# First stage of a decoder layer: rows of three engines' queues put in another order

## The chip, the cores and the metric

The kernel runs on one NeuronCore of a Trainium2 chip. The metric is the time of one execution on the device in microseconds (us). Five engines each work through their own queue of instructions strictly in order, and semaphores tie them together: PE (TensorE: matrix products and transposes), DVE (VectorE), ACT (ScalarE), POOL (GpSimd) and SP (SyncE, which here only issues DMA transfers).

## The reference

One decoder layer in float32 on x of shape (2, 512, 1024). Only its first third bears on the change:

```
h   = (x - mean(x)) / sqrt(var(x) + 1e-5)          # each row of 1024
q   = h @ Wq.T                                      # 32 heads of 128
lat = [h @ Wk_down.T, h @ Wv_down.T]                # 256 + 256 columns, by kv head
k, v = lat[:256] @ Wk_up.T, lat[256:] @ Wv_up.T     # 8 kv heads of 128
x   = x + softmax(causal(q @ k.T / sqrt(128))) @ v @ Wo.T
x   = x + layernorm(x) times a quantised context    # second part
x   = x + routed low-rank FFN of layernorm(x)       # third part
```

## The kernel before

The 1024 rows of x are eight tiles of 128 rows (TT = 8; tile t lies in x_sb[:, t, :]). A float32 operand of a product is kept as two float16 parts, a high and a low one, and a product is three matmuls for each piece of 128 along the contraction (high x high, high x low, low x high; the helper split_product, L1551).

**The first stage** normalises the tiles, turns them and multiplies them with the down projections. For one tile t the steps are:

1. DVE takes statistics (two bn_stats of 512 columns at L1112, then L1114 and L1115, which signals var_done). POOL raises var + eps to the power -1/2 (L618, pow_done). DVE refines that in three steps and makes the bias (ln1_rstd, L1123 to L1131, rstd_done).
2. ACT writes the normalised tile into one of two buffers (ln1_apply, L831, ln_done; it needs the transposes of tile t - 2 behind it).
3. PE turns it with eight transposes into two PSUM banks (columns, L1565, ln_turned).
4. ACT copies the two banks to float16 high parts (columns_hi, ht_hi), and DVE makes the low parts from bank and high part (columns_lo, ht_lo). The tile in the profile is h_b, or wo_in for the first half of the columns of tiles 4 to 7.

**The down projection** has four blocks of weights (DOWN = 4), each 128x1024. ACT makes the high part of block n (down_hi, wo_hi) and DVE the low part (down_lo, wo_lo); both are written to wo_sb. PE walks pairs of tiles: in pair p (tiles 2p and 2p + 1) it makes the product with block hp = 0, 1, 2, 3, each of 24 matmuls of 256 columns. Before hp 0 it waits until the low parts of both tiles are there. In pair 0 it also waits for the low part of each block. The transposes of later tiles are put between: before hp 0 and hp 1 those of tiles 2p + 2 and 2p + 3.

**Latents.** After pairs 0 and 1 the four products of the first batch are whole. For each block ACT (latent_hi, L823) and DVE (latent_lo, L1153) copy them out as float16 parts in four pieces of 64x256 (tile o_t in the profile); pairs 2 and 3 write the same PSUM banks again, so hp n of pair 2 waits for the copy of block n. Block 0 is copied in step t = 5 of the loops of ACT and DVE, blocks 1, 2 and 3 in step t = 6 (down_heads). In the loops before the change the refinement of tile t + 2 stands behind the low parts of tile t, so that of tile 7 stands in step 5.

After this stage come the k and v projections, the first queries, and then eight groups of four heads, in which PE is fed by all the others.

The order in the queues is written out by hand. DVE's and ACT's are the loops over t at the end of their first part, PE's is the loop over pairs.

Of the kernel before, what the change touches and what calls it, by code (L numbers as in the profile page):

```python
# [14 lines left out]
TT = TOK // P  # L15
# [5 lines left out]
HALF = 512  # L21
# [79 lines left out]
DOWN = 4  # L101
# [90 lines left out]
def decoder_layer(nc, x, ctx_in, wq, wdown, wup, wo, a_w, b_w, router_w, keys, quant, ctx_whole, b_whole, kv_whole, out):  # L192
# [8 lines left out]
    with ctx:  # L201
        ps = ctx.enter_context(nc.psum_tensor("ps", [P, 8, HALF], F32))
        x_sb = sb("x_sb", [P, TT, DIM], F32)
# [19 lines left out]
        stats = sb("stats", [P, 3 * TT, 2, 6], F32)  # L223
# [76 lines left out]
        x_loaded = [sem(f"x_loaded{n}") for n in range(TT)]  # L300
# [445 lines left out]
        def _(act):  # L746
# [65 lines left out]
            def columns_hi(t):  # L812
                for j in range(2):
                    act.wait_ge(ln_turned, 2 * t + j + 1)
                    split_hi(h_block(t // QT, j)[:, 0, :, t % QT * P:(t % QT + 1) * P],
                             ps[:, 2 * (t % 2) + j, :].rearrange("p (k n) -> p k n", k=4), ht_hi, S_H)

            def latent_hi(b, hp):
                act.wait_ge(gen_done, b * DOWN + hp + 1)
                for half in range(2):  # L820
                    for j in range(2):
                        src, (hi, _) = latent_views(b, hp, half, j)
                        ins = nc.scalar.activation(hi, src, ACT.Copy, scale=LAT_OUT)  # L823
                ins.then_inc(gen_hi, 1)

            def ln1_apply(t):
                if t >= 2:

                    act.wait_ge(ln_turned, 2 * (t - 1))
                act.wait_ge(rstd_done, t + 1)  # L830
                nc.scalar.activation(hn[:, t % 2, :], x_sb[:, t, :], ACT.Identity, bias=ln_bias[:, t:t + 1],  # L831
                                     scale=rstd1[:, 2, t:t + 1]).then_inc(ln_done, 1)

            def down_hi(n):
                act.wait_ge(down_loaded[n], 16)
                split_hi(wo_sb[:, n, 0, :], down_in[:, n, :], wo_hi, S_W)

            down_hi(0)
            for t in range(2):
                ln1_apply(t)  # L840
            for t in range(TT):
                if t in (5, 6):
                    for hp in down_heads(t):
                        latent_hi(0, hp)
                columns_hi(t)
                if t + 2 < TT:
                    ln1_apply(t + 2)
                if t + 1 < DOWN:
                    down_hi(t + 1)
            def up_split(n):  # L850

                act.wait_ge(up_loaded[n % 3], 16 * (n // 3 + 1))
# [202 lines left out]
            for i in range(0, TT + STEPS_AHEAD):  # L1055
                if 0 <= i - 1 < TT:
                    t = i - 1
# [12 lines left out]
                if 0 <= i - 1 < TT:  # L1070
                    t = i - 1
# [17 lines left out]
                if 0 <= i - 1 < TT:  # L1089
                    t = i - 1  # L1090
# [4 lines left out]
        def _(dve):  # L1095
            newtons = [0]

            def link(ins):
                newtons[0] += 1
                ins.then_inc(newton, 1)  # L1100
                dve.wait_ge(newton, newtons[0])
# [6 lines left out]
            def ln_stats(k, t):  # L1108

                n = k * TT + t  # L1110
                for j in range(2):
                    ins = nc.vector.bn_stats(stats[:, n, j, :], x_sb[:, t, j * HALF:(j + 1) * HALF])  # L1112
                link(ins)
                link(nc.vector.bn_aggr(mean_var[:, n, :], stats[:, n, :, :].rearrange("p a b -> p (a b)")))  # L1114
                nc.vector.tensor_scalar(var_eps[:, n:n + 1], mean_var[:, n, 1:2], EPS, None, ALU.add).then_inc(var_done, 1)  # L1115
                variances[0] += 1
                return variances[0]
# [11 lines left out]
            def ln1_rstd(t, turn):  # L1129
                link(ln_rstd(0, t, turn))  # L1130
                nc.vector.scalar_tensor_tensor(ln_bias[:, t:t + 1], mean_var[:, t, 0:1], -1.0, rstd1[:, 2, t:t + 1],  # L1131
                                               ALU.mult, ALU.mult).then_inc(rstd_done, 1)

            def ln1_stats(t):
                dve.wait_ge(x_loaded[t], 16)
                return ln_stats(0, t)
# [5 lines left out]
            def columns_lo(t):  # L1142
                for j in range(2):
                    dve.wait_ge(ht_hi, 2 * t + j + 1)
                    hi, lo = (h_block(t // QT, j)[:, part, :, t % QT * P:(t % QT + 1) * P] for part in range(2))
                    split_lo(lo, ps[:, 2 * (t % 2) + j, :].rearrange("p (k n) -> p k n", k=4), hi, ht_lo, S_H)

            def latent_lo(b, hp):
                dve.wait_ge(gen_hi, b * DOWN + hp + 1)
                for half in range(2):  # L1150
                    for j in range(2):
                        src, (hi, lo) = latent_views(b, hp, half, j)
                        ins = nc.vector.scalar_tensor_tensor(lo, src, LAT_OUT, hi, ALU.mult, ALU.subtract)  # L1153
                ins.then_inc(gen_read, 1)

            def down_lo(n):
                dve.wait_ge(wo_hi, n + 1)
                split_lo(wo_sb[:, n, 1, :], down_in[:, n, :], wo_sb[:, n, 0, :], wo_lo, S_W)

            turns = {t: ln1_stats(t) for t in range(2)}  # L1160
            for t in range(2):
                ln1_rstd(t, turns[t])
            down_lo(0)
            turns[2] = ln1_stats(2)
            for t in range(TT):
                if t in (5, 6):
                    for hp in down_heads(t):
                        latent_lo(0, hp)
                columns_lo(t)
                if t + 2 < TT:  # L1170
                    ln1_rstd(t + 2, turns[t + 2])
                if t + 1 < DOWN:
                    down_lo(t + 1)
                if t + 3 < TT:
                    turns[t + 3] = ln1_stats(t + 3)
            def block_split(place, slot, number):

                dve.wait_ge(wq_hi, number)
# [364 lines left out]
        def _(pe):  # L1543
# [27 lines left out]
            for pair in range(PAIRS):  # L1571

                b, part = pair // 2, pair % 2
                at = part * 2 * P
                for hp in range(DOWN):
                    if hp < 2 and 2 * pair + 2 + hp < TT:
                        columns(2 * pair + 2 + hp)
                    if hp == 0:
                        pe.wait_ge(ht_lo, 4 * (pair + 1))
                    if pair == 0:  # L1580
                        pe.wait_ge(wo_lo, hp + 1)
                    if b == 1 and part == 0:

                        pe.wait_ge(gen_read, hp + 1)
                    ins = split_product(ps[:, DOWN_BANK[hp], part * 2 * P:(part + 1) * 2 * P],
                                        [(lambda i, k=k: wo_sb[:, hp, i, k * P:(k + 1) * P],
                                          lambda j, k=k: h_block(b, k // 4)[:, j, k % 4, at:at + 2 * P])
                                         for k in range(KT)])
                    if part == 1:
                        ins.then_inc(gen_done, 1)  # L1590
# [349 lines left out]
```

## Time and profile before

| what | value |
|---|---|
| median of 3 runs | 1127.27 us (1125.13 to 1130.5) |
| the profiled execution | 1127.93 us, span in the profile 1126.2 us |
| PE busy | 1078.6 us, 96% of the span |
| DVE, ACT, POOL busy | 904.5, 536.3, 411.7 us |
| mean granted clock of TensorE | 0.991 |
| first stage | from 0 to about 69 us |

The profiled execution is 0.66 us above the median of the runs; 1.73 us of it lie outside the span. "Busy" of PE counts pipelined matmuls, so it tells where PE had work, not how fast it went. A row with x24 is 24 instructions that followed each other. The granted clock is given as a share of 2.4 GHz: 1.00 is 2.4 GHz, 0.50 is 1.2 GHz. In the first 25 us that column reads 1.00 while matmuls of the same shape take twice the time that they take later, so there the durations are what tells the clock.

### The profile page before, as it was taken

What the parts mean: (1) busy time and instruction counts of PE and PEld (TensorE: products, weight loads), DVE (VectorE), ACT (ScalarE), POOL (GpSimd) and SP (SyncE); (2) the same over time, 40 slices, a digit from 0 to 9 for tenths busy, and PEclk for the clock granted to TensorE, in tenths of its full rate; (3) what the DMA queues carried; (4) which work ended last, traced back from release to release, by engine and by line L of the source; (5) the groups of instructions that cost most, each with busy time, mean ns of one, the idle gap of its engine ahead of it and who ended that gap; (6) DMA issues with size and microseconds to landing.
All of it is one profiled execution on the core that took longest, in us unless ns stands there. A gap on an engine that the chain in (4) does not pass through costs nothing.

```text
span 1126.2 us, 19872 instructions
## 1 busy us (share of the span) xinstructions
PE 1078.6 (96%) x6361; PEld 581.5 (52%) x6368; DVE 904.5 (80%) x1868; ACT 536.3 (48%) x1094; POOL 411.7 (37%) x423
## 2 busy tenths in 40 slices
PE   4999988999999999999999999999999989799998
PEld 3876544555555555555555555555555544344554
DVE  6789588988787978888887978788888897867753
ACT  4656366545454545455454445454455460342421
POOL 2049655544343534424453434344243340000000
PEclk9999999999999999999999999999999999899999
DMA  8026146654454545455544544554554576000001
GB/s 310 1 79 231 75 89 155 144 138 100 117 133 112 131 123 135 102 119 131 132 103 121 133 112 112 141 131 102 123 131 98 139 200 211 1 1 38 20 38 56
DMA packets 200865, 128.66 MB, mean 114 GB/s; under 512 B 171376, under 2 KB 173552, under 8 KB 199920
## 3 DMA queue, kind: packets, MB, share of 16 engines
q1 hardware_dynamic: 200816, 128.03, 43.6%
q8 instruction: 28, 0.46, 0.2%
q14 instruction: 21, 0.17, 0.1%
HBM read 68.23 MB, written 17.83 MB: 76 GB/s over the span
## 4 chain that ended last, share of the span: by engine, by line
PE 81%; DVE 10%; ACT 5%; issue 2%; DMA 1%; POOL 0%; SPq 0%; ACTq 0%; DVEq 0%; POOLq 0%
PE ps L1551 77%; PE ps L1802 2%; ACT prob L975 1%; DVE stats L1112 1%; DVE wo_sb L1104 1%; DVE h_b L1104 1%; DVE prob L1310 1%; DVE x_sb L1486 1%; DVE x_sb L1468 1%; DVE prob_t L1104 1%; DMA o_t<-in_wdown 1%; ACT prob L1034 1%; PE ps L1565 0%; ACT q_t L1049 0%; ACT side_out L1039 0%
## 5 line engine op out<-in xcount | busy, mean ns | idle before, releaser
L712 POOL TENSOR_SCALAR prob<-prob,row_inv 128x128 f32<-128x128 f32 (+3 forms) x256 | 203.5, 815 | 438.7 <-DVE row_inv L1281 438.7
L1551 PE MATMUL ps<-wo_sb,o_t 128*128 128x512 f16 x1536 | 353.0, 380 | 3.6 <-DVE x_sb L1292 3.6
L1551 PE MATMUL ps<-h_b,wq_sb 128*128 128x512 f16 x1524 | 343.2, 381 | 0.0
L975 ACT ACTIVATE prob<-prob,neg_max 128x128 f32<-128x128 f32 (+3 forms) x256 | 140.6, 550 | 221.7 <-DVE neg_max L1316 221.7
L1551 PEld LDWEIGHTS ps<-h_b,wq_sb 128*128 128x128 f16 x1524 | 148.9, 98 | 179.2 <-issue 3.7
L1551 PEld LDWEIGHTS ps<-wo_sb,o_t 128*128 128x128 f16 x1536 | 147.6, 98 | 173.1 <-DVE x_sb L1292 6.3
L1292 DVE SCALAR_TENSOR_TENSOR x_sb<-ps,x_sb 128x512 f32<-128x512 f32 x256 | 174.0, 685 | 54.9 <-PE ps L1551 54.1
L1551 PE MATMUL ps<-prob_t,v_sb 128*128 128x128 f16 (+2 forms) x960 | 116.4, 274 | 5.6 <-DMA prob_t<-prob_s 5.6
L1551 PE MATMUL ps<-k_t,q_t 128*128 128x512 f16 (+3 forms) x768 | 114.8, 299 | 1.9 <-DVE neg_max L1316 1.8
L1310 DVE CUSTOM_DVE_ANT_0 prob<-ps,mask 128x512 f32<-128x512 f32 (+3 forms) x256 | 110.2, 483 | 2.3 <-issue 1.6
L1551 PEld LDWEIGHTS ps<-prob_t,v_sb 128*128 128x128 f16 x960 | 83.4, 98 | 35.9 <-DMA prob_t<-prob_s 6.5
L748 ACT ACTIVATE q_t<-q_tmp 128x512 f16<-128x512 f32 x60 | 37.8, 630 | 131.7 <-DVE q_tmp L1268 131.7
L1268 DVE SCALAR_TENSOR_TENSOR q_tmp<-ps,q_tmp 128x512 f32<-128x512 f32 x105 | 72.0, 686 | 29.9 <-PE ps L1551 27.4
L1104 DVE SCALAR_TENSOR_TENSOR prob_s<-prob,prob_s 128x1280 f16<-128x1280 f32 x64 | 95.0, 1484 | 0.1
L1551 PEld LDWEIGHTS ps<-k_t,q_t 128*128 128x128 f16 x768 | 66.9, 98 | 53.0 <-issue 2.3
L748 ACT ACTIVATE prob_s<-prob 128x1280 f16<-128x1280 f32 x64 | 80.6, 1259 | 27.6 <-POOL prob L712 27.6
L1104 DVE SCALAR_TENSOR_TENSOR wq_sb<-wq_in,wq_sb 128x512 f16<-128x512 f32 x94 | 67.4, 731 | 0.5 <-ACT wq_sb L748 0.5
L742 POOL TENSOR_TENSOR rstd<-var_eps,minus_half 128x1 f32<-128x1 f32 x16 | 8.8, 550 | 155.3 <-DVE var_eps L1115 155.3
L1104 DVE SCALAR_TENSOR_TENSOR q_t<-q_tmp,q_t 128x512 f16<-128x512 f32 x60 | 62.1, 1056 | 0.7 <-ACT q_t L748 0.7
L1104 DVE SCALAR_TENSOR_TENSOR o_t<-ps,o_t 128x512 f16<-128x512 f32 x64 | 44.2, 691 | 20.1 <-ACT o_t L748 20.1
L748 ACT ACTIVATE wq_sb<-wq_in 128x512 f16<-128x512 f32 x94 | 56.5, 618 | 3.0 <-POOL wq_in L671 3.0
L975 ACT ACTIVATION_READ_ACCUMULATOR prob<-prob,neg_max 128x1 f32 x256 | 47.8, 187 | 0.0
(141 smaller groups left out, 1175.0 us busy)
## 6 DMA issues: line engine op xcount, KB each, us to landing
wq_in<-in_wq SPq DMA_DIRECT2D x64, 256.0 KB, 3.4
wo_in<-in_wo SPq DMA_DIRECT2D x32, 512.0 KB, 3.8
side_in<-in_ctx SPq DMA_DIRECT2D x16, 512.0 KB, 4.4
kv_parts<-wo_sb SPq DMA_DIRECT2D x7, 1024.0 KB, 5.7
x_sb<-in_x SPq DMA_DIRECT2D x8, 512.0 KB, 9.0
ctx_quantised<-side_out SPq DMA_DIRECT2D x16, 256.0 KB, 2.9
h_b<-ctx_quantised SPq DMA_DIRECT2D x2, 2048.0 KB, 10.8
out<-x_sb SPq DMA_DIRECT2D x8, 512.0 KB, 2.6
```

What stands on the lines that cost most here:

```text
L712: ins = nc.gpsimd.tensor_scalar(at, at, row_inv[:, u % 2, q:q + 1], S_P, ALU.mult, ALU.mult)
L748: nc.scalar.activation(dst, src, ACT.Copy, scale=scale).then_inc(signal, 1)
L975: ins = nc.scalar.activation(at, at, ACT.Exp, bias=neg_max[:, n % 2, q:q + 1], scale=SOFTMAX, accum_out=row_sum[:, n % 2, q:q + 1])
L1034: nc.scalar.activation(hn[:, t % 2, :], x_sb[:, t, :], ACT.Identity, bias=x_bias[:, t:t + 1], scale=x_scale[:, 1, t:t + 1]).then_inc(x_aff ...
L1104: nc.vector.scalar_tensor_tensor(dst, src, scale, hi, ALU.mult, ALU.subtract).then_inc(signal, 1)
L1112: ins = nc.vector.bn_stats(stats[:, n, j, :], x_sb[:, t, j * HALF:(j + 1) * HALF])
L1268: nc.vector.scalar_tensor_tensor(q_tmp[:, dst, :], ps[:, Q_BANK[product % 2], :], Q_OUT, q_tmp[:, src, :], ALU.mult, ALU.add).then_inc(com ...
L1292: nc.vector.scalar_tensor_tensor(at, ps[:, bank, :], WO_OUT, at, ALU.mult, ALU.add).then_inc(wo_read, 1)
L1310: ins = nc.vector.tensor_tensor_reduce(prob[:, u % 2, at:at + width], ps[:, at // HALF, at % HALF:at % HALF + width], mask[:, SEQ - width: ...
L1468: nc.vector.scalar_tensor_tensor(x_sb[:, t, :], column_term[:, b, :], row_term[:, t:t + 1], x_sb[:, t, :], ALU.add, ALU.add).then_inc(x_fo ...
L1551: ins = nc.tensor.matmul(out_, lhs(i), rhs(j), start=start and n == 0, stop=stop and n == 3 * len(pairs) - 1)
L1802: ins = nc.tensor.matmul(ps[:, x_banks(t)[j], :], x_qt[:, t % 2, k * P:(k + 1) * P], ctx_q[:, b, k, j * HALF:(j + 1) * HALF], start=k == 0 ...
```

## The change

On DVE the statistics can now be taken in halves (ln1_half, ln1_end). The statistics of tile 1 are split around the refinement of tile 0. Behind the low part of down block 0 stand one half of the statistics of tile 2 and then the low parts of tiles 0 and 1; the rest of tile 2, tile 3 and the blocks 1 to 3 follow. From tile 4 on DVE's loop refines tile t + 1 (before: t + 2) ahead of the low parts of tile t, and takes the statistics of tile t + 2 (before: t + 3). ACT's queue is put in the order that goes with it: tile 0 is normalised ahead of the high part of down block 0, and from step 4 on tile t + 1 is normalised ahead of the high parts of tile t. PE makes the first down product of pair 0 before it turns tile 2, and turns tile 3 ahead of hp 2. No arithmetic is added or taken away.

```diff
@@ -835,18 +835,26 @@
                 act.wait_ge(down_loaded[n], 16)
                 split_hi(wo_sb[:, n, 0, :], down_in[:, n, :], wo_hi, S_W)
 
+            ln1_apply(0)
             down_hi(0)
-            for t in range(2):
-                ln1_apply(t)
-            for t in range(TT):
+            ln1_apply(1)
+            columns_hi(0)
+            columns_hi(1)
+            down_hi(1)
+            ln1_apply(2)
+            down_hi(2)
+            columns_hi(2)
+            ln1_apply(3)
+            down_hi(3)
+            columns_hi(3)
+            ln1_apply(4)
+            for t in range(4, TT):
                 if t in (5, 6):
                     for hp in down_heads(t):
                         latent_hi(0, hp)
+                if t + 1 < TT:
+                    ln1_apply(t + 1)
                 columns_hi(t)
-                if t + 2 < TT:
-                    ln1_apply(t + 2)
-                if t + 1 < DOWN:
-                    down_hi(t + 1)
             def up_split(n):
 
                 act.wait_ge(up_loaded[n % 3], 16 * (n // 3 + 1))
@@ -1111,6 +1119,9 @@
                 for j in range(2):
                     ins = nc.vector.bn_stats(stats[:, n, j, :], x_sb[:, t, j * HALF:(j + 1) * HALF])
                 link(ins)
+                return ln_variance(n)
+
+            def ln_variance(n):
                 link(nc.vector.bn_aggr(mean_var[:, n, :], stats[:, n, :, :].rearrange("p a b -> p (a b)")))
                 nc.vector.tensor_scalar(var_eps[:, n:n + 1], mean_var[:, n, 1:2], EPS, None, ALU.add).then_inc(var_done, 1)
                 variances[0] += 1
@@ -1157,22 +1168,46 @@
                 dve.wait_ge(wo_hi, n + 1)
                 split_lo(wo_sb[:, n, 1, :], down_in[:, n, :], wo_sb[:, n, 0, :], wo_lo, S_W)
 
-            turns = {t: ln1_stats(t) for t in range(2)}
-            for t in range(2):
-                ln1_rstd(t, turns[t])
+            def ln1_half(t, j):
+                dve.wait_ge(x_loaded[t], 16)
+                return nc.vector.bn_stats(stats[:, t, j, :], x_sb[:, t, j * HALF:(j + 1) * HALF])
+
+            def ln1_end(t):
+                link(ln1_half(t, 1))
+                return ln_variance(t)
+
+            ln1_half(0, 0)
+            turns = {0: ln1_end(0)}
+            ln1_half(1, 0)
+            ln1_rstd(0, turns[0])
+            turns[1] = ln1_end(1)
+            ln1_rstd(1, turns[1])
             down_lo(0)
-            turns[2] = ln1_stats(2)
-            for t in range(TT):
+            ln1_half(2, 0)
+            columns_lo(0)
+            columns_lo(1)
+            turns[2] = ln1_end(2)
+            ln1_half(3, 0)
+            ln1_rstd(2, turns[2])
+            down_lo(1)
+            turns[3] = ln1_end(3)
+            down_lo(2)
+            ln1_rstd(3, turns[3])
+            columns_lo(2)
+            down_lo(3)
+            turns[4] = ln1_stats(4)
+            columns_lo(3)
+            ln1_rstd(4, turns[4])
+            turns[5] = ln1_stats(5)
+            for t in range(4, TT):
                 if t in (5, 6):
                     for hp in down_heads(t):
                         latent_lo(0, hp)
+                if t + 1 < TT:
+                    ln1_rstd(t + 1, turns[t + 1])
                 columns_lo(t)
                 if t + 2 < TT:
-                    ln1_rstd(t + 2, turns[t + 2])
-                if t + 1 < DOWN:
-                    down_lo(t + 1)
-                if t + 3 < TT:
-                    turns[t + 3] = ln1_stats(t + 3)
+                    turns[t + 2] = ln1_stats(t + 2)
             def block_split(place, slot, number):
...
@@ -1573,8 +1608,9 @@
                 b, part = pair // 2, pair % 2
                 at = part * 2 * P
                 for hp in range(DOWN):
-                    if hp < 2 and 2 * pair + 2 + hp < TT:
-                        columns(2 * pair + 2 + hp)
+                    turned_here = 2 * pair + 2 + hp - (pair == 0)
+                    if (1 <= hp <= 2 if pair == 0 else hp < 2) and turned_here < TT:
+                        columns(turned_here)
                     if hp == 0:
                         pe.wait_ge(ht_lo, 4 * (pair + 1))
                     if pair == 0:
```

DVE, from the low part of down block 0 (wo_sb) on; h_b are low parts of turned tiles, BN_STATS are halves of the statistics. Before:

```order
L1104 SCALAR_TENSOR_TENSOR wo_sb<-o_t,wo_sb 128x1024
L1112 BN_STATS stats<-x_sb 128x6 x2
L1114 BN_AGGR mean_var<-stats 128x2
L1115 TENSOR_SCALAR var_eps<-mean_var 128x1
L1104 SCALAR_TENSOR_TENSOR h_b<-ps,h_b 128x4x128 x2
L1123 TENSOR_TENSOR rstd1<-rstd0 128x1
L1124 TENSOR_SCALAR rstd1<-rstd1,var_eps 128x1
L1126 SCALAR_TENSOR_TENSOR rstd1<-rstd1,rstd0 128x1
L1131 SCALAR_TENSOR_TENSOR ln_bias<-mean_var,rstd1 128x1
L1104 SCALAR_TENSOR_TENSOR wo_sb<-o_t,wo_sb 128x1024
```

And the same place now:

```order
L1112 SCALAR_TENSOR_TENSOR wo_sb<-o_t,wo_sb 128x1024
L1173 BN_STATS stats<-x_sb 128x6
L1112 SCALAR_TENSOR_TENSOR h_b<-ps,h_b 128x4x128 x4
L1173 BN_STATS stats<-x_sb 128x6
L1125 BN_AGGR mean_var<-stats 128x2
L1126 TENSOR_SCALAR var_eps<-mean_var 128x1
L1173 BN_STATS stats<-x_sb 128x6
L1134 TENSOR_TENSOR rstd1<-rstd0 128x1
L1135 TENSOR_SCALAR rstd1<-rstd1,var_eps 128x1
L1137 SCALAR_TENSOR_TENSOR rstd1<-rstd1,rstd0 128x1
L1142 SCALAR_TENSOR_TENSOR ln_bias<-mean_var,rstd1 128x1
L1112 SCALAR_TENSOR_TENSOR wo_sb<-o_t,wo_sb 128x1024
```

The low parts of both first tiles (x4) now stand together and ahead of the variance of tile 2; before, those of tile 1 stood another block, another tile's statistics and a refinement later.

DVE, steps 5 and 6 of its loop; o_t x4 are the latents of block 0, o_t x12 those of blocks 1 to 3, wo_in and h_b the low parts of a tile, rstd1 and ln_bias a refinement. Before:

```order
L1153 SCALAR_TENSOR_TENSOR o_t<-ps,o_t 64x4x64 x4
L1104 SCALAR_TENSOR_TENSOR wo_in<-ps,wo_in 128x4x128
L1104 SCALAR_TENSOR_TENSOR h_b<-ps,h_b 128x4x128
L1123 TENSOR_TENSOR rstd1<-rstd0 128x1
L1124 TENSOR_SCALAR rstd1<-rstd1,var_eps 128x1
L1126 SCALAR_TENSOR_TENSOR rstd1<-rstd1,rstd0 128x1
L1131 SCALAR_TENSOR_TENSOR ln_bias<-mean_var,rstd1 128x1
L1153 SCALAR_TENSOR_TENSOR o_t<-ps,o_t 64x4x64 x12
```

And now, from the low parts of tile 5 on:

```order
L1112 SCALAR_TENSOR_TENSOR wo_in<-ps,wo_in 128x4x128
L1112 SCALAR_TENSOR_TENSOR h_b<-ps,h_b 128x4x128
L1120 BN_STATS stats<-x_sb 128x6 x2
L1125 BN_AGGR mean_var<-stats 128x2
L1126 TENSOR_SCALAR var_eps<-mean_var 128x1
L1164 SCALAR_TENSOR_TENSOR o_t<-ps,o_t 64x4x64 x12
L1134 TENSOR_TENSOR rstd1<-rstd0 128x1
L1135 TENSOR_SCALAR rstd1<-rstd1,var_eps 128x1
L1137 SCALAR_TENSOR_TENSOR rstd1<-rstd1,rstd0 128x1
L1142 SCALAR_TENSOR_TENSOR ln_bias<-mean_var,rstd1 128x1
```

The refinement of tile 7 stood ahead of the twelve latent pieces and now stands behind them. On ACT the normalising of tile 7 (L831) has moved likewise:

```order
L748 ACTIVATE wo_in<-ps 128x4x128
L748 ACTIVATE h_b<-ps 128x4x128
L823 ACTIVATE o_t<-ps 64x4x64 x12
L831 ACTIVATE prob<-x_sb,ln_bias,rstd1 128x1024
L748 ACTIVATE wo_in<-ps 128x4x128
L748 ACTIVATE h_b<-ps 128x4x128
```

These are the rows of the changed kernel: tile 5's high parts, the latents, tile 7 normalised, tile 6's high parts. Before, L831 stood ahead of the twelve o_t.

## Rows read from the trace of the kernel before

**Rows 1.** the page: its first line, and the chain that ended last by line

```profile
span 1126.2 us, 19872 instructions
...
PE ps L1551 77%; PE ps L1802 2%; ACT prob L975 1%; DVE stats L1112 1%; DVE wo_sb L1104 1%; DVE h_b L1104 1%; DVE prob L1310 1%; DVE x_sb L1486 1%; DVE x_sb L1468 1%; DVE prob_t L1104 1%; DMA o_t<-in_wdown 1%; ACT prob L1034 1%; PE ps L1565 0%; ACT q_t L1049 0%; ACT side_out L1039 0%
```

**Rows 2.** the waits, 0 to 62 us: engine, line, releaser; us in total, times, longest

```profile
ACT prob L831 <- DVE ln_bias L1131: 17.7, 6, 3.9
...
PE ps L1565 <- ACT prob L831: 11.6, 2, 9.9
```

**Rows 3.** timeline, 0 to 10 us: start us, us, engine, line, operation, count [idle before]

```profile
5.97 0.56 POOL L618 TENSOR_TENSOR rstd<-var_eps,minus_half 128x1 f32<-128x1 f32 x1 [2.07 <-DVE var_eps L1115]
...
7.52 1.06 ACT L748 ACTIVATE wo_sb<-o_t 128x1024 f16<-128x1024 f32 x1 [5.51 <-DMA o_t<-in_wdown]
...
8.49 2.36 ACT L831 ACTIVATE prob<-x_sb,ln_bias,rstd 128x1024 f32<-128x1024 f32 x2
...
9.86 3.64 PE L1565 MATMUL ps<-ident,prob 128*128 128x128 f32 x16 [9.86 <-ACT prob L831]
```

**Rows 4.** timeline, 16 to 26 us

```profile
16.17 1.23 DVE L1104 SCALAR_TENSOR_TENSOR wo_sb<-o_t,wo_sb 128x1024 f16<-128x1024 f32 x1 [2.32 <-ACT wo_sb L748]
17.32 1.28 DVE L1112 BATCH_NORM_STATS2 stats<-x_sb 128x6 f32<-128x512 f32 x2
...
18.94 1.28 DVE L1104 SCALAR_TENSOR_TENSOR h_b<-ps,h_b 128x512 f16<-128x512 f32 x2
19.10 0.55 POOL L618 TENSOR_TENSOR rstd<-var_eps,minus_half 128x1 f32<-128x1 f32 x1 [6.73 <-DVE var_eps L1115]
20.14 0.15 DVE L1123 TENSOR_TENSOR rstd<-rstd 128x1 f32<-128x1 f32 x1
...
20.28 4.90 PE L1551 MATMUL ps<-h_b,wo_sb 128*128 128x256 f16 x24 [3.06 <-DVE h_b L1104]
...
21.02 1.24 ACT L831 ACTIVATE prob<-x_sb,ln_bias,rstd 128x1024 f32<-128x1024 f32 x1 [3.91 <-DVE ln_bias L1131]
22.16 1.04 ACT L748 ACTIVATE wo_sb<-o_t 128x1024 f16<-128x1024 f32 x1
23.11 1.06 ACT L748 ACTIVATE h_b<-ps 128x512 f16<-128x512 f32 x2
...
25.01 1.04 PE L1565 MATMUL ps<-ident,prob 128*128 128x128 f32 x8
```

**Rows 5.** timeline of PE alone, 38 to 52 us

```profile
38.58 8.02 PE L1551 MATMUL ps<-h_b,wo_sb 128*128 128x256 f16 x72
46.44 1.04 PE L1565 MATMUL ps<-ident,prob 128*128 128x128 f32 x8
...
49.94 1.04 PE L1565 MATMUL ps<-ident,prob 128*128 128x128 f32 x8
50.81 1.47 PE L1551 MATMUL ps<-wo_in,wo_sb 128*128 128x256 f16 x12
```

**Rows 6.** timeline, 40 to 54 us: latents on DVE

```profile
41.70 1.73 DVE L1153 SCALAR_TENSOR_TENSOR o_t<-ps,o_t 64x256 f16<-64x256 f32 x4 [1.18 <-ACT o_t L823]
...
48.26 5.25 DVE L1153 SCALAR_TENSOR_TENSOR o_t<-ps,o_t 64x256 f16<-64x256 f32 x12 [2.81 <-ACT o_t L823]
```

**Rows 7.** timeline of PE alone, 168 to 190 us

```profile
170.93 2.97 PE L1551 MATMUL ps<-prob_t,v_sb 128*128 128x128 f16 x15 [2.97 <-DMA prob_t<-prob_s]
173.69 5.90 PE L1551 MATMUL ps<-h_b,wq_sb 128*128 128x512 f16 x24
...
183.29 1.81 PE L1551 MATMUL ps<-prob_t,v_sb 128*128 128x128 f16 x15 [2.07 <-DMA prob_t<-prob_s]
184.94 5.34 PE L1551 MATMUL ps<-h_b,wq_sb 128*128 128x512 f16 x24
```

**Rows 8.** windows: busy by engine (count), granted clock, DMA share, GB/s

```profile
170.90:173.70 2.80, 2.77 (x16) 1.77 (x17) 2.10 (x3) 0.82 (x2) 2.80 (x3) 0.59 0.65 246
...
983.20:986.00 2.80, 2.80 (x8) 0.92 (x7) 2.63 (x9) 0.20 (x1) 0.62 (x2) 0.50 0.00 0
```

## The prediction

> **What bounds the kernel now.** I read the page first. Its span is 1126.2 us and 77% of the chain that ended last is one line of matmuls [rows 1], so PE sets the time nearly everywhere, and a microsecond that PE starts later or earlier is kept unless something absorbs it. Then the waits of the first 62 us: PE waits 11.6 us for its first normalised tiles, and ACT waits six times, 17.7 us in all, for the bias that DVE makes [rows 2]. So early on PE is fed by a relay DVE, POOL, DVE, ACT, PE. The timeline shows the relay. Products start at 20.28 us, after an idle of 3.06 us, when the second low part of tile 1 is done (18.94 + 1.28); that low part stands behind a down block and the statistics of tile 2 [rows 4]. Later PE leads: from 38.58 us it runs 72 matmuls, then transposes, without a wait, and turns tile 7 at 49.94 us with no idle before it [rows 5].
>
> **Prices, from one row to the next on the same engine** [rows 4]. DVE: low part of a down block 1.15 us (16.17 to 17.32), statistics with variance 1.62 (17.32 to 18.94), low parts of a tile 1.20 (18.94 to 20.14). From the first step of a refinement to the start of the normalising on ACT 0.88 (20.14 to 21.02); DVE itself is free about 0.1 earlier than that, so 0.75. POOL: the power ends 0.71 after the instruction that follows the variance has begun (18.94 to 19.65). ACT: normalising 1.24 long, 1.14 to the next; high part of a block 0.95. Latents: 1.7 per block on DVE, 5.1 to 5.25 for three [rows 6]. PE: eight transposes step by 0.87 (49.94 to 50.81), a product of 24 matmuls by 2.62 ((46.44 - 38.58) / 3) [rows 5]; at the slow clock 1.82 (3.64 / 2) [rows 3] and 4.9 [rows 4].
>
> **Part 1, the start: the first product comes about 5.8 us earlier.** The power of tile 0 is there at 5.97 + 0.56 = 6.53; DVE now refines at once and ACT normalises at about 7.45. Before, it stood behind the high part of block 0 and began at 8.49 [rows 3]. The refinement pushes the statistics of tile 1 back; its variance comes at about 8.4, its power at 9.0, and it is normalised at about 9.95 (before 8.49 + 1.14 = 9.63). PE turns tile 0 from 8.8 (before 9.86) and tile 1 from 11.2 to 13.1. The low parts of tiles 0 and 1 follow at once and end at about 14.45. First product: 14.5 instead of 20.28.
>
> **Part 2, pairs 0 and 1: 4.6 us are kept.** The first product goes at the slow clock, 14.5 to 19.4, as it did before (4.90 us, 204 ns a matmul) [rows 4]. With tiles 2 and 3 turned (2 x 0.87) and three products at 2.62, pair 0 ends at about 29.0. DVE's queue meanwhile: rest of tile 2 and half of tile 3 to 15.5, power 16.1, tile 2 normalised 17.0; block 1 to 18.0; variance 3 by 19.1; block 2 from 19.25 (it waits for ACT) to 20.4; refinement 3, tile 3 normalised 21.3; low parts of tile 2 to 22.3; block 3, whose high part ACT makes only behind tile 3, 23.5 to 24.65 (a DVE wait of 1.2); statistics of tile 4 to 26.25; low parts of tile 3 to 27.45; tile 4 normalised 28.3 to 29.6. So PE waits 0.6 us for tile 4, turns it at 29.7, and begins pair 1 at 30.5; with tile 5 turned in it pair 1 ends at 30.5 + 0.87 + 4 x 2.62 = 41.85. Before it ended at 46.44. That is 4.6 us.
>
> **Part 3, tile 7: a new wait takes it back.** DVE's refinement of tile 7 now stands behind the latents of blocks 1 to 3, and ACT's normalising likewise. I follow DVE on: statistics 5 to 29.8, power 30.5, tile 5 normalised 31.4; its high parts queue behind that on ACT, 32.6, so the low parts of tile 4 run 33.2 to 34.4 (a wait of 1.9); statistics 6 to 36.0; latents of block 0 to 37.7; refinement 6, tile 6 normalised 38.6 to 39.85; only then high parts of tile 5, and low parts from 40.4 to 41.6 (again 1.9); statistics 7 to 43.2; twelve latent pieces to 48.3; refinement 7 and the hand-over 0.88; tile 7 normalised 49.2 to 50.45. PE turns it at 50.6. PE has meanwhile turned tile 6 and made the first product of pair 2, and stands idle from about 45.35: **5.2 us**. Behind this wait stand seven products of the stage and all that follows. The transposes of tile 7 began at 49.94 before [rows 5], so the first stage is then 0.6 to 0.8 us late, not 4.6 early; I take **+0.7**. The error of the walk is that of some 25 hand-overs rounded to 0.05; I allow 0.7 on either side.
>
> **Part 4, the clock.** After an idle of 2.97 us at 168 to 170.93 PE was slow: 15 matmuls took 2.97 us, which took 1.81 at 183.29 behind an idle of 2.07, and the next 24 took 5.90 against 5.34 [rows 7]; the granted clock was 0.59 in that stretch and 0.50 from 983.2 to 986 [rows 8], which is 1.2 GHz. That cost 1.16 + 0.56 = 1.7 us. The first product lost 4.90 - 2.62 = 2.3 us. The new idle is longer than either of the idles before them. Lower bound of its price: 0, if the clock stays. Upper: 3.2, tile 7 at 1.82 instead of 0.87 and one whole product at 4.9 instead of 2.62. I take 2.0, between the two measured losses. The Trainium skill, "TensorE: Matmul & The Clock Gate", section "Part 4: PE-mode transpose", says that the full clock does not engage for transposes. The trace disagrees: eight transposes took 1.04 us at 25.01 [rows 4] and half of 3.64 in [rows 3]. By the rule the turning of tile 7 would be no cheaper at the fast clock and the price would lose 0.95; I go by the rows.
>
> **What is hidden.** The low parts of tile 7 end at about 53.4, ahead of pair 3, so PE doesn't wait there. The splitting of statistics costs nothing: same instructions, and DVE has the waits named above. No DMA is moved, and the transfers of x are hardly wanted earlier: the statistics of tile 3 begin at 15.5 us instead of 17.32 [rows 4]. Nothing behind the stage waits on an absolute time: k, v and queries start from the latents of PE's last products.
>
> **Sum.** -5.8 at the start, +1.2 by pair 1 (the wait for tile 4 and the other order), +5.3 at tile 7, +2.0 for the clock: **+2.7 us**. Against the profiled execution's own 1127.93 us that is 1130.6; the median of the runs lies 0.66 below it, so 1130.0 us on that scale, 0.24% more.
>
> **Rivals.**
> - The wait comes but the clock stays: +0.7, 1128.0. For it: the idle of 2.07 us at 183.29 left the clock alone [rows 7]. Against: this one is over twice as long.
> - Absorbed: DVE, whose work on tile 7 is done 2.5 us earlier than before, and later stages make good what PE lost; about 0, 1127.3. For it: in the relay of the softmax PE waits for DMA, not for itself (2.97 and 2.07 us) [rows 7]. Against: those transfers start from scores that PE computed, so they move with it.
> - No wait at tile 7, the start's gain is kept: -4.6 plus nothing, 1122.7. It needs PE to get tile 7 by 45.35, that is DVE and ACT 5 us faster over three tiles. The twelve latent pieces alone are 5.1 us of queue, so only a mistake of mine in the queues gives this.
> - The other side, clearly slower: the clock stays low over many products after the wait. At half clock every microsecond of old work costs one more, so from 5 us of work (two products) on the loss with the wait passes 5.7 us and the time 1133. For it: at 983 to 986 the clock was still 0.50 well into the work [rows 8]. Against: the first product ended it within 4.9 us [rows 4]. A slow clock that lasts into the transposes of tile 2 adds up to 0.95 too, of which 0.2 is slack.
>
> **Chances.** Forecast (wait and clock, 1129 to 1132) 0.58; clock stays 0.12; absorbed 0.15; gain kept 0.06; long slow clock 0.09. An effect under 0.5% (5.6 us) can't be told from no change here. The forecast, clock-stays and absorbed cases all lie within it, and so does most of the gain-kept case (4.6 us): same 0.89. The long slow clock is mostly beyond: slower 0.08. Faster 0.03. The range 1125.8 to 1133.0 holds the first three cases with the runs' own spread (1125.13 to 1130.5) and the near end of the fourth, and leaves the ends of the others out.
>
> **What would show it.** Right: products start near 14.5 us; the last of pair 1 ends near 42; a wait PE <- ACT prob (normalising) of about 5 us ends near 50.6; transposes and matmuls behind it take twice the usual time; the k and v stage, which began at 50.81 + 7 x 2.62 = 69.15 [rows 5], begins near 71.9. Wrong in part 1: first product after 16. Wrong in part 3: a wait under 3 us, or the refinement of tile 7 done before 46. Wrong in part 4: 24 matmuls behind the wait in 2.8 us. Wrong in "hidden": PE's stage ends 2.7 late but the span does not grow by it.

## The result, and the profile after

The changed kernel takes 1129.49 us in the median of 20 runs (1128.19 to 1131.62), the kernel before 1127.41 us (1125.07 to 1130.63, 20 runs). The ratio is 1.0019 with a 95% interval of 1.0011 to 1.0028: 2.1 us slower, between 1.2 and 3.2. The forecast was 2.7 us slower, 1130.0 us. The interval excludes zero, so 20 runs did tell an effect that the prediction held for too small to be told, and it excludes the +0.7 us of the rival in which the clock stays.

The page's first line and the chain by line answer to [rows 1]; the products' share of the chain has fallen from 77% to 76%.

```profile
span 1127.5 us, 19879 instructions
...
PE ps L1586 76%; PE ps L1838 2%; DVE stats L1120 2%; ACT prob L983 1%; DVE h_b L1112 1%; DVE prob L1345 1%; DVE wo_sb L1112 1%; DVE o_t L1164 1%; DVE x_sb L1503 1%; ACT prob L831 1%; DVE x_sb L1521 1%; ACT prob L1042 1%; DVE prob_t L1112 1%; ACT side_out L1047 1%; ACT q_t L1057 0%
```

The waits of the first 62 us answer to [rows 2] (engine, line, releaser; us in total, times, longest). PE waits 16.7 us for normalised tiles where it waited 11.6, and six times instead of twice. The third line is new among the large ones: DVE waits for high parts that ACT makes.

```profile
ACT prob L831 <- DVE ln_bias L1142: 22.4, 8, 5.3
PE ps L1600 <- ACT prob L831: 16.7, 6, 8.7
...
DVE wo_in L1112 <- ACT wo_in L748: 5.8, 3, 2.0
```

PE's timeline answers to the PE rows of [rows 3 to 5]. The columns are start, us, engine, line, operation, count, and in brackets the idle time before it and what ended it.

```profile
8.69 1.94 PE L1600 MATMUL ps<-ident,prob 128*128 128x128 f32 x8 [8.69 <-ACT prob L831]
11.10 1.77 PE L1600 MATMUL ps<-ident,prob 128*128 128x128 f32 x8 [0.47 <-ACT prob L831]
14.28 2.79 PE L1586 MATMUL ps<-h_b,wo_sb 128*128 128x256 f16 x24 [1.42 <-DVE h_b L1112]
18.11 1.09 PE L1600 MATMUL ps<-ident,prob 128*128 128x128 f32 x8 [1.03 <-ACT prob L831]
...
22.36 1.09 PE L1600 MATMUL ps<-ident,prob 128*128 128x128 f32 x8 [0.54 <-ACT prob L831]
...
29.43 1.09 PE L1600 MATMUL ps<-ident,prob 128*128 128x128 f32 x8 [0.74 <-ACT prob L831]
...
33.85 8.02 PE L1586 MATMUL ps<-h_b,wo_sb 128*128 128x256 f16 x72
41.71 1.04 PE L1600 MATMUL ps<-ident,prob 128*128 128x128 f32 x8
...
50.64 1.97 PE L1600 MATMUL ps<-ident,prob 128*128 128x128 f32 x8 [5.27 <-ACT prob L831]
52.40 2.02 PE L1586 MATMUL ps<-wo_in,wo_sb 128*128 128x256 f16 x12
54.25 1.47 PE L1586 MATMUL ps<-h_b,wo_sb 128*128 128x256 f16 x12
...
71.28 1.03 PE L1586 MATMUL ps<-o_t,prob_t 128*128 128x512 f16 x4
```

The first product begins at 14.28 instead of 20.28 us. Tiles 2, 3 and 4 are waited for (1.03, 0.54, 0.74). Tile 6 is turned at 41.71 instead of 46.44: PE is 4.7 us ahead. Then it is idle for 5.27 us and turns tile 7 at 50.64 instead of 49.94, 0.70 late. The transposes take 1.97 us instead of 1.04, the next twelve matmuls step by 1.85 instead of 1.31, and k and v begin at 71.28 instead of 69.15, **2.13 us late**.

What DVE and ACT do meanwhile (timeline of all engines, answers to [rows 6]):

```profile
32.98 0.69 DVE L1112 SCALAR_TENSOR_TENSOR wo_in<-ps,wo_in 128x512 f16<-128x512 f32 x1 [1.85 <-ACT wo_in L748]
...
40.35 0.69 DVE L1112 SCALAR_TENSOR_TENSOR wo_in<-ps,wo_in 128x512 f16<-128x512 f32 x1 [1.99 <-ACT wo_in L748]
...
43.18 5.24 DVE L1164 SCALAR_TENSOR_TENSOR o_t<-ps,o_t 64x256 f16<-64x256 f32 x12
...
48.45 0.16 DVE L1134 TENSOR_TENSOR rstd<-rstd 128x1 f32<-128x1 f32 x1
...
49.34 1.24 ACT L831 ACTIVATE prob<-x_sb,ln_bias,rstd 128x1024 f32<-128x1024 f32 x1 [3.97 <-DVE ln_bias L1142]
```

DVE waits 1.85 and 1.99 us for the high parts of tiles 4 and 5, makes twelve latent pieces in 5.24 us, and only then refines tile 7. ACT, which has been idle for 3.97 us, normalises it at 49.34.

The windows tell the clock (busy time of PE, PEld, DVE, ACT and POOL with counts, then granted clock, DMA share, GB/s):

```profile
45.20:50.40 5.20, 0.17 (x2) 0.00 (x0) 3.80 (x12) 1.23 (x2) 0.00 (x0) 0.97 0.00 0
...
50.80:53.00 2.20, 2.20 (x11) 1.99 (x12) 1.76 (x3) 1.85 (x4) 0.00 (x0) 0.50 0.00 0
```

Behind the idle the granted clock is 0.50, that is 1.2 GHz, as in [rows 8].

**Where the 2.1 us are after that.** Late in the program, with the same work in both kernels, the kernel before:

```profile
927.95 7.04 PE L1551 MATMUL ps<-wo_sb,o_t 128*128 128x512 f16 x24 [2.41 <-DVE x_sb L1292]
```

```profile
976.22 1.32 PE L1888 MATMUL ps<-ident,k_t 128*128 128x128 f32 x8 [3.40 <-ACT k_t L1066]
```

and the changed one:

```profile
931.79 5.35 PE L1586 MATMUL ps<-wo_sb,o_t 128*128 128x512 f16 x24 [2.41 <-DVE x_sb L1327]
```

```profile
978.39 1.91 PE L1924 MATMUL ps<-ident,k_t 128*128 128x128 f32 x8 [3.40 <-ACT k_t L1074]
```

The last rows of each (the first transposes for the routed part) stand 2.17 us apart, nearly the 2.13 of the start of k and v. It did not stay at that in between, and the near equality is luck: two events of the clock cancel. At 183 us the lag was 2.15 (185.44 against 183.29 in [rows 7]). There the changed kernel ran slow where the kernel before did not (2.29 and 6.59 us where that took 1.81 and 5.34), and it lost another 1.7:

```profile
185.44 2.29 PE L1586 MATMUL ps<-prob_t,v_sb 128*128 128x128 f16 x15 [2.16 <-DMA prob_t<-prob_s]
187.52 6.59 PE L1586 MATMUL ps<-h_b,wq_sb 128*128 128x512 f16 x24
```

So the rows at 928 and 932 stand 3.84 us apart. There it is the other way round: behind the same idle of 2.41 us the kernel before ran 24 matmuls mostly at the slow clock (7.04 us), the changed one at the fast clock (5.35). Of the eight kernels below, five ran them fast in the profiled run and three slow. Apart from these two events the lag of 2.1 us is carried through 900 us. The two spans differ by only 1.3 us, as near 995 us the clock differs once more; the 20 runs each give 2.1.

### The profile page after: what moved, and what is told of

Its sections match the earlier page's. It is cut to its first block, busy times and chain, and to the rows that moved or that the text cites. A ratio compares the mean times of both kernels' runs of the same rounds, so it can differ in the third digit from the quotient of the medians.

```text
span 1127.5 us, 19879 instructions
## 1 busy us (share of the span) xinstructions
PE 1077.5 (96%) x6368; PEld 580.8 (52%) x6368; DVE 905.2 (80%) x1868; ACT 536.8 (48%) x1094; POOL 411.1 (36%) x423
## 4 chain that ended last, share of the span: by engine, by line
PE 79%; DVE 12%; ACT 5%; issue 2%; POOL 1%; DMA 0%; ACTq 0%; DVEq 0%; POOLq 0%; SPq 0%
PE ps L1586 76%; PE ps L1838 2%; DVE stats L1120 2%; ACT prob L983 1%; DVE h_b L1112 1%; DVE prob L1345 1%; DVE wo_sb L1112 1%; DVE o_t L1164 1%; DVE x_sb L1503 1%; ACT prob L831 1%; DVE x_sb L1521 1%; ACT prob L1042 1%; DVE prob_t L1112 1%; ACT side_out L1047 1%; ACT q_t L1057 0%
## 5 line engine op out<-in xcount | busy, mean ns | idle before, releaser
L1112 DVE SCALAR_TENSOR_TENSOR wq_sb<-wq_in,wq_sb 128x512 f16<-128x512 f32 x94 | 67.6, 733 | 0.5 <-ACT wq_sb L748 0.3
```

Of the source, the lines that this page charges most:

```text
L1112: nc.vector.scalar_tensor_tensor(dst, src, scale, hi, ALU.mult, ALU.subtract).then_inc(signal, 1)
```

## The experiments

All were timed in five rounds beside the kernel before. "k and v" is the start of the k and v projections in the profiled run, 69.15 us before and 71.28 with the change; a ratio is to the kernel before on the same chip. A ratio is not the quotient of the two medians: for the best kernel the ratio says 4.6 us less and the medians 3.7. A landmark is that of one profiled run. Before any wait that an edit touches it moves by itself: in the seven traces that have the change's start and PE's new order (the change among them) the first product begins between 14.21 and 14.59 us, so differences under 0.4 us are not read from one landmark.

| kernel | idle at tile 7, us | k and v, us | median, us | ratio (95%) |
|---|---|---|---|---|
| the change | 5.27 | 71.28 | 1129.49 | 1.0019 (1.0011 to 1.0028) |
| DVE refines tile 7 first | 1.30 | 66.25 | 1123.47 | 0.9974 (0.9964 to 0.9984) |
| and ACT: tile 7 between latents | 0.74 | 65.56 | 1123.23 | 0.9962 (0.9951 to 0.9974) |
| the wait filled with matmuls | 0.88 | 70.10 | 1128.03 | 1.0010 (0.9996 to 1.0024) |
| before, tile 7 moved alone | 2.06 | 71.29 | 1130.77 | 1.0029 (1.0014 to 1.0044) |
| tile 7 ahead of all latents | 0.73 | 69.11 | 1125.21 | 0.9997 (0.9987 to 1.0007) |
| tile 7 between, high parts first | none | 64.34 | 1122.23 | 0.9959 (0.9946 to 0.9972) |
| the change, high parts first | 2.26 | 68.74 | 1123.75 | 0.9981 (0.9972 to 0.9989) |
| the change, old PE order | 4.22 | 75.00 | 1130.96 | 1.0042 (1.0029 to 1.0055) |

The first four experiments ran beside a kernel before of 1126.98 us, the other four beside one of 1125.9; ratios compare across the two groups, medians do not.

### Take the new wait away: DVE alone

```diff
             for t in range(4, TT):
+                if t == 6:
+                    ln1_rstd(7, turns[7])
                 if t in (5, 6):
                     for hp in down_heads(t):
                         latent_lo(0, hp)
-                if t + 1 < TT:
+                if t + 1 < TT and t != 6:
                     ln1_rstd(t + 1, turns[t + 1])
```

> The changed kernel, and on DVE alone the refinement of tile 7 put ahead of the latents of blocks 1 to 3 (ACT as in the change). Theory (the new wait at tile 7 is what took the head start back): ACT normalises tile 7 as soon as its own latents are done, about 45.3 us; PE turns tile 7 at about 46.6 behind an idle of about 1.3 us instead of 5.3, the clock stays, k and v begin near 68 instead of 71.3 us, and the time is 3 to 3.5 us below the kernel before (about 1124.2) and 5 to 5.5 below the change. Rival (the later stages don't carry a head start, DVE sets their pace): the wait goes, k and v begin earlier, but the time is within 1 us of the kernel before. Rival (the loss lies in the new start itself): as slow as the change, 1129.5.

Measured: 0.26% below the kernel before (2.9 us), 0.45% below the change. PE's timeline:

```profile
46.98 1.09 PE L1602 MATMUL ps<-ident,prob 128*128 128x128 f32 x8 [1.30 <-ACT prob L831]
...
66.25 1.46 PE L1588 MATMUL ps<-o_t,prob_t 128*128 128x512 f16 x6
```

The idle is 1.30 us, as expected, and the turning is at 46.98 (46.6 expected; this run began 0.3 us later); the clock stays (transposes 1.09). k and v begin at 66.25 us, where the expectation said 68: that number was a slip, since 3 us less than 69.15 is 66. Four instructions of refinement in another place of one queue are worth 5 us, 1.4 of it the clock. The rival by which later stages don't carry a head start falls, and so does the one that puts the loss in the new start.

### And ACT between the latents

```diff
                     for hp in down_heads(t):
+                        if hp == 3:
+                            ln1_apply(7)
                         latent_hi(0, hp)
-                if t + 1 < TT:
+                if t + 1 < TT and t != 6:
                     ln1_apply(t + 1)
```

> As the run before, and on ACT tile 7 is normalised ahead of the latents of block 3 instead of behind them. Theory: tile 7 is turned at about 46.2, idle about 0.8 us, k and v begin near 67.6, and the time is 3.6 to 4 us below the kernel before (about 1123.7), 0.5 below the run before. Rival (head start not carried): within 1 us of the kernel before.

```profile
44.10 0.16 DVE L1136 TENSOR_TENSOR rstd<-rstd 128x1 f32<-128x1 f32 x1 [0.66 <-POOL rstd L618]
...
44.82 5.24 DVE L1166 SCALAR_TENSOR_TENSOR o_t<-ps,o_t 64x256 f16<-64x256 f32 x12
45.00 1.24 ACT L831 ACTIVATE prob<-x_sb,ln_bias,rstd 128x1024 f32<-128x1024 f32 x1 [1.02 <-DVE ln_bias L1144]
...
46.29 1.09 PE L1604 MATMUL ps<-ident,prob 128*128 128x128 f32 x8 [0.74 <-ACT prob L831]
```

DVE waits only for POOL's power, refines tile 7 at 44.10, and makes the twelve latent pieces behind that; ACT normalises at 45.00, PE turns the tile at 46.29. k and v begin at 65.56, 3.6 us before the kernel before (the 67.6 of the expectation has the same slip). The ratio 0.9962 is 4.3 us less (2.9 to 5.5). The 0.5 us expected against the run before can't be told from the times, as the intervals overlap; the timelines show 0.69, of which 0.12 is an earlier start.

### Fill the wait

```diff
+                    if pair == 2 and hp == 1:
+                        pe.wait_ge(ht_lo, 12)
+                        for n in range(40):
+                            nc.tensor.matmul(ps[:, 3, 0:2 * P], wo_sb[:, 0, 0, 0:P], h_b[:, 0, 0, 0, 0:2 * P],
+                                             start=True, stop=True)
                     if (1 <= hp <= 2 if pair == 0 else hp < 2) and turned_here < TT:
                         columns(turned_here)
```

> The changed kernel with 40 extra matmuls of 256 columns on PE in the wait for tile 7, into the bank that its transposes write afterwards; nobody reads what they write. They take about 4.4 us (40 x 0.109) of the 5.3 us of idle. Theory (of the 2.1 us that the change lost, 0.7 is lateness of tile 7 and 1.4 the slow clock behind the idle): tile 7 is turned at the same 50.6 us but in 1.04 instead of 1.97 us, the first 24 matmuls behind it take 2.8, k and v begin near 69.9, and the time is 0.7 above the kernel before (about 1128.1), 1.4 below the change. Rival (the clock is not what slows it there): no less than the change, 1129.5.

```profile
45.42 4.53 PE L1615 MATMUL ps<-h_b,wo_sb 128*128 128x256 f16 x40
50.83 1.09 PE L1600 MATMUL ps<-ident,prob 128*128 128x128 f32 x8 [0.88 <-ACT prob L831]
51.76 1.47 PE L1586 MATMUL ps<-wo_in,wo_sb 128*128 128x256 f16 x12
...
70.10 1.46 PE L1586 MATMUL ps<-o_t,prob_t 128*128 128x512 f16 x6
```

```profile
45.20:50.40 5.20, 4.75 (x44) 4.00 (x41) 4.00 (x12) 1.23 (x2) 0.00 (x0) 1.00 0.00 0
...
50.80:53.00 2.20, 2.17 (x20) 2.03 (x21) 1.57 (x3) 2.20 (x5) 0.00 (x0) 1.00 0.05 11
```

Tile 7 comes just as late (50.83, in a run whose first product began 0.2 us later), but its transposes take 1.09 us and the next matmuls step at full speed; the granted clock is 1.00 in both windows in which the change showed 0.97 and 0.50. k and v begin at 70.10, 0.95 us late instead of 2.13. The ratio is 1.1 us above the kernel before (0.5 fewer to 2.7 more), which can't separate the expected 0.7 from 0, nor from the 2.1 of the change: by time alone the rival (the clock is not what slows it) stands. What decides is the rows: with the wait filled the slow matmuls are gone, and in the change the lag at k and v splits into lateness and clock, 2.13 = 0.70 + 1.43.

### Only tile 7, in the kernel before

```diff
@@ ACT
+                if t == 6:
+                    ln1_apply(7)
                 columns_hi(t)
-                if t + 2 < TT:
+                if t + 2 < TT and t != 5:
                     ln1_apply(t + 2)
@@ DVE
+                if t == 6:
+                    ln1_rstd(7, turns[7])
                 columns_lo(t)
-                if t + 2 < TT:
+                if t + 2 < TT and t != 5:
                     ln1_rstd(t + 2, turns[t + 2])
```

> The kernel before with one thing of the change: DVE refines and ACT normalises tile 7 behind the latents of blocks 1 to 3. Theory (the order alone makes the wait): without the head start the latents of block 3 wait for PE; tile 7 is normalised at about 50.7 and turned at about 52.1 us behind an idle of about 2.2 us, k and v begin 2.0 to 2.3 us later than before, near 71.3, plus up to 1.5 if the clock falls; time 1129.4 to 1131. Rival (the wait comes from the other moves, not from this one): as before, 1127.4.

```profile
15.10 1.09 PE L1569 MATMUL ps<-ident,prob 128*128 128x128 f32 x8 [1.75 <-ACT prob L831]
...
52.02 1.09 PE L1569 MATMUL ps<-ident,prob 128*128 128x128 f32 x8 [2.06 <-ACT prob L831]
52.95 1.47 PE L1555 MATMUL ps<-wo_in,wo_sb 128*128 128x256 f16 x12
...
71.29 1.46 PE L1555 MATMUL ps<-o_t,prob_t 128*128 128x512 f16 x6
```

Idle 2.06, turned at 52.02, k and v at 71.29: 2.14 us late, nearly the same as the whole change. The parts differ, so the near equality is chance: here it is all lateness, as the clock stayed behind this idle, and there it is 0.70 of lateness and 1.43 of clock. The one move is enough to lose as much as the whole change, and the rest of the change makes a gain that it hides.

By the ratio this kernel is 3.3 us slower (1.6 to 5.0). The profiled run is not typical of it: it took 1127.43 us, one of three at 1127.2 to 1127.6, while the other nine took 1129.4 to 1132.8. Its lag is still 2.4 us at 928 (its matmuls there begin at 930.36) and goes only behind that, first of all where the kernel before took 7.04 us for the 24 matmuls and this one 5.35. Whether the clock fell behind the wait in the nine slower runs is not shown; the trace is of another run.

### Tile 7 ahead of all latents

```diff
@@ ACT; DVE as in the first experiment
+                if t == 6:
+                    ln1_apply(7)
                 if t in (5, 6):
                     for hp in down_heads(t):
                         latent_hi(0, hp)
-                if t + 1 < TT:
+                if t + 1 < TT and t != 6:
                     ln1_apply(t + 1)
```

> The changed kernel with tile 7's refinement on DVE and its normalising on ACT both put ahead of all three latents of step 6, which is the old order at that place. Theory (the wait moves to whoever stands behind tile 7): tile 7 is turned at about 46.3 us, but ACT makes the high latents of block 1 only behind it, 46 to 47.6, DVE the low ones to 49.3, and PE waits about 2.4 us for block 1 ahead of the second product of pair 2. k and v begin near 68, 1.2 us before the kernel before; time about 1126. Rival (whatever takes tile 7 out of the way of PE gives the whole head start): as in the run with tile 7 between blocks 2 and 3, 1123.2.

```profile
46.27 1.09 PE L1604 MATMUL ps<-ident,prob 128*128 128x128 f32 x8 [0.73 <-ACT prob L831]
49.47 2.74 PE L1590 MATMUL ps<-wo_in,wo_sb 128*128 128x256 f16 x12 [2.11 <-DVE o_t L1166]
```

The wait moves as expected: 0.73 us at tile 7, then 2.11 us for the latents of block 1, whose high parts stand behind tile 7 on ACT. What the expectation left out is the clock: the twelve matmuls behind it took 2.74 us instead of 1.47, and the 24 of that product 1.3 us more than usual. k and v begin at 69.11, not 68, and the ratio is 0.9997 (within 1.5 us of the kernel before): the whole head start is gone again.

### High parts first, with tile 7 between and alone

```diff
+                columns_hi(t)
                 if t + 1 < TT and t != 6:
                     ln1_apply(t + 1)
-                columns_hi(t)
```

> The best version so far (DVE refines tile 7 ahead of the latents, ACT normalises it ahead of block 3's) and on ACT the high parts of tile t ahead of the normalising of tile t + 1 in steps 4 to 7. Theory: the two waits of DVE for high parts (1.85 and 1.99 us) go, tile 7 is normalised at about 42 us, and PE has no wait for it (0.74 before); k and v begin near 64.8 us, the time is 0.7 to 0.8 below that version (about 1122.4). Rival (nothing left there): 1123.2. Theory of a loss (tile 5 to 7 are normalised later and PE waits for them): a PE wait of over 1 us in pair 1 or 2 and over 1124.

```profile
45.12 1.04 PE L1604 MATMUL ps<-ident,prob 128*128 128x128 f32 x8
...
64.34 1.46 PE L1590 MATMUL ps<-o_t,prob_t 128*128 128x512 f16 x6
```

PE turns tile 7 at 45.12 without a wait and k and v begin at 64.34 us, 4.8 earlier than in the kernel before. The ratio 0.9959 (4.6 us less, 3.2 to 6.1, from five runs) is the lowest of all; against the version without this edit (0.9962) the intervals can't tell it apart, the timeline gains 1.2 us, 0.9 of it the gap ahead of tile 7 and most of the rest an earlier start (14.21 instead of 14.47).

With the same edit for tiles 4 and 5 alone, and tile 7 left behind the latents:

> The changed kernel and only one thing else: on ACT the high parts of tiles 4 and 5 ahead of the normalising of tiles 5 and 6. Tile 7 is still refined behind all latents. Theory (the wait at tile 7 has two parts: DVE's two waits for high parts, 3.8 us, and the place behind the latents): DVE is earlier until it meets the latents of block 3, which wait for PE's own last product of pair 1; tile 7 is normalised at about 46.3 and turned at 47.6 behind an idle of about 2.2 us; k and v begin near 67; time about 1125. Rival (only the place behind the latents counts): no change, 1129.5.

```profile
47.80 1.89 PE L1603 MATMUL ps<-ident,prob 128*128 128x128 f32 x8 [2.26 <-ACT prob L831]
49.49 2.38 PE L1589 MATMUL ps<-wo_in,wo_sb 128*128 128x256 f16 x12
```

The idle falls by 3.0 us, from 5.27 to 2.26, and tile 7 is turned at 47.80, as expected. Both of DVE's waits for high parts, 3.84 us together, are gone; a new one of 0.81 for the latents of block 0 gives the rest. In the profiled run the clock fell all the same (1.89, then 2.38 for twelve, 1.7 us in all), and k and v began at 68.74 (67 expected); that run took 1127.41 us, the slowest of its eleven, whose median is 1123.75. The rival (only the place behind the latents counts) falls: 2.8 to 3.0 us of the lateness came from ACT's order in steps 4 and 5.

### The change with PE's old order

```diff
-                    turned_here = 2 * pair + 2 + hp - (pair == 0)
-                    if (1 <= hp <= 2 if pair == 0 else hp < 2) and turned_here < TT:
-                        columns(turned_here)
+                    if hp < 2 and 2 * pair + 2 + hp < TT:
+                        columns(2 * pair + 2 + hp)
```

> The changed kernel with PE's old order: tile 2 is turned ahead of the first down product, tile 3 ahead of the second. Theory (while tile 7 binds, PE's own head start is idle time): the first product begins at about 19 us instead of 14.3, pair 1 ends 1.5 to 2 us later, the idle at tile 7 shrinks by as much to about 4 us, tile 7 is turned at 50.6 to 51.1 and k and v begin 71.3 to 71.8; time 1129.5 to 1130, as the change. Rival (every microsecond that PE loses at the start counts): 2 us above the change, 1131.5.

Measured: 0.42% above the kernel before. My theory is wrong here. PE's timeline, and DVE's waits:

```profile
18.29 1.97 PE L1600 MATMUL ps<-ident,prob 128*128 128x128 f32 x8 [5.24 <-ACT prob L831]
20.05 4.73 PE L1586 MATMUL ps<-h_b,wo_sb 128*128 128x256 f16 x24
...
33.35 1.04 PE L1600 MATMUL ps<-ident,prob 128*128 128x128 f32 x8
...
53.46 1.97 PE L1600 MATMUL ps<-ident,prob 128*128 128x128 f32 x8 [4.22 <-ACT prob L831]
...
75.00 1.46 PE L1586 MATMUL ps<-o_t,prob_t 128*128 128x512 f16 x6
```

```profile
34.62 0.69 DVE L1112 SCALAR_TENSOR_TENSOR wo_in<-ps,wo_in 128x512 f16<-128x512 f32 x1 [3.33 <-ACT wo_in L748]
...
38.62 1.73 DVE L1164 SCALAR_TENSOR_TENSOR o_t<-ps,o_t 64x256 f16<-64x256 f32 x4 [1.09 <-ACT o_t L823]
...
43.17 0.69 DVE L1112 SCALAR_TENSOR_TENSOR wo_in<-ps,wo_in 128x512 f16<-128x512 f32 x1 [1.99 <-ACT wo_in L748]
```

PE idles 5.24 us for tile 2, turns it and makes the first product at the slow clock (4.73 us), and turns tile 4 at 33.35 instead of 29.43. DVE then waits 3.33 us for the high parts of tile 4 (1.85 with the change) and 1.09 more for the latents of block 0, and tile 7 is turned at 53.46, 2.82 later than in the change; 1.48 and 1.09 of it are these two. The slow clock behind the wait costs 0.9 more than in the change, and together that is the 3.7 us by which k and v are later. The relay behind tile 7 thus begins at PE's transposes of tile 4: of the 5.8 us that the first product lost, 3.9 reach tile 4 and 2.8 tile 7. PE's head start was in part idle time, not as a whole. The rival, that all of it counts, isn't met either. The first product also took 4.73 us here, where the change had 2.79; the expectation does not name that.

## Why the prediction was right

**The start** (-5.8 us forecast, -6.0 measured: 14.28 against 20.28). The chain of refinement, normalising, turning and low parts came out within 0.25 us at every step. One assumption failed: that the first product goes at the slow clock. It took 2.79 us, not 4.9. It made no difference, as PE then waited 1.03 and 0.54 us for tiles 2 and 3, which it would have spent in the product. That is luck: the price was wrong and slack took it up. Four of the kernels with the same start show it: there the product took 4.08 to 4.51 us, and tile 4 was turned 15.1 us after the product began, as here (29.43 - 14.28).

**Pairs 0 and 1** (4.6 ahead; 46.44 - 41.71 = 4.73). The wait for tile 4 was 0.74 (0.6 forecast), DVE's for block 3 1.12 (1.2), its two for high parts 1.85 and 1.99 (1.9 each).

**Tile 7** (wait of 5.2 us ending at 50.6, +0.7; measured 5.27, 50.64, +0.70). The moved refinement was the cause: moved alone it costs 2.14 us of the stage, moved back on DVE it gives 5.0.

**The clock** (2.0 forecast, 1.43 measured). This is the term that was mis-sized: 0.89 in the transposes (a step of 1.76 instead of 0.87) and 0.54 in the first twelve matmuls. I took it between two losses of 1.7 and 2.3, from [rows 7] and [rows 4]; it was below both. Filling the wait took 1.2 us of it back. The upper bound of 3.2 had a whole product at the slow clock; in the trace only part of its first twelve matmuls was.

**Hidden, and absorbed.** The low parts of tile 7 ended at 53.95 (53.4 forecast), well ahead of pair 3 at 60.80, and PE did not wait for them. Nothing gave the loss back: apart from the clock the lag of 2.1 us is carried to 978, and the 20 runs have it too, so the rival "absorbed" falls; the one with the clock unmoved is the filled wait, not the change; the long slow clock did not come.

The sum was -5.8 + 1.2 + 5.3 + 2.0 = 2.7; the trace has -6.00 + 1.27 + 5.43 + 1.43 = 2.13, the runs 2.1 (1.2 to 3.2). The range of 1125.8 to 1133.0 also held two rivals (clock stays, absorbed) and the near end of a third, so the time alone would not have shown the mechanism; the landmarks do. The size of the rival in which the gain is kept, -4.6 us, is what the best version measures by its ratio (3.7 by the medians); only, it takes edits of two queues to get it.

## What to carry to other kernels

Where in-order queues feed each other, an item that is early enough for its consumer before a change may not be so after it: when a head start is made at one end, walk every queue to the point where it would be used up, and look for the one item that slid behind a long block (here four tiny instructions behind 5.2 us of copies). A wait on TensorE can cost more than its length: where the clock fell behind one in this stage, the work behind it took 1.3 to 2.3 us more, and behind waits of 1.30 and 2.06 us it took nothing. An order that serves the next consumer first, with the copies split around it, kept the head start (k and v 4.8 us early, where PE was 4.7 ahead at tile 6); putting that consumer ahead of everything moved the wait to the next one.

## What the runs showed of the hardware

In these traces the length of an idle of about 2 us does not tell whether the clock stays. Behind 2.06 us it stayed (transposes 1.09 us), behind 2.26 it fell (1.89) and behind 2.11, with 0.73 shortly before, it fell (2.74 for twelve matmuls); behind 2.41 late in the program it fell in the kernel before and stayed in the changed one. Kernels whose code is the same up to there differ too: in the kernel with tile 7 moved alone, tile 2, at 15.10 us, was turned in 1.09 us where the kernel before took 1.97 at 15.25. The runs of one kernel, five to twenty of each, spread by 1.6 to 5.6 us; so an effect of 2 us needs many runs, or a landmark in the timeline ahead of the places where the clock goes either way.
